# Halving eight products in each of the last three rows of a streamed fp32 matrix product, and moving VectorE's running totals to PSUM

## The chip, the core and the metric

The kernel runs on one core of one Trainium2 chip. The metric is the device time of one execution in microseconds (us), as the median of several runs. A core has the engines TensorE (PE in the profile; its weight loads are PEld), VectorE (DVE), ScalarE (ACT), GpSimd (POOL) and SyncE (SP), which here only issues loads. They run their own instruction lists in order and meet through semaphores. SBUF and PSUM are the on-chip memories; TensorE writes to PSUM alone, which has eight banks of 512 fp32 values in each of 128 partitions.

## The reference

A graph layer with an 8192 x 8192 matrix A and an 8192 x 128 matrix x. The part that the change touches is the first product.

```python
def _lap_mul(A, x):
    d = 1.0 / jnp.sqrt(jnp.sum(A, axis=-1))
    return d[:, None] * (A @ (d[:, None] * x))
z = _lap_mul(A, x) @ W1 + b1
z = jax.nn.leaky_relu(z, negative_slope=0.1)
...
S = jnp.where(ranks < k, S, 0.0)      # similarities of z, the 4 nearest of each row
A2 = S + A
out = _lap_mul(A2, x) @ W2 + b2       # then x + out, layer norm
```

All of it is fp32. A row's scale d is known only when the whole row of A has been summed.

## The kernel before

A comes in 16 x 16 quads of 512 rows x 512 columns, 1 MB each, transposed on the host to tiles of 128 x 4 x 512. The first stage streams all 256 quads through SBUF once, row block by row block (16 quads each; "row b" below is a row block of 512 rows, "quad (b, q)" its columns of block q).

- SP (L665, L666) loads quad after quad into slots of 1 MB. A slot is loaded again once VectorE has added its quad and TensorE has done its product, if it has one. `next_slot` picks the slot; the last twelve loads of the stage (`STREAM_END`) use six slots only.
- VectorE adds the row's 16 quads into `total`, a 128 x 2048 tile in SBUF (`add_quad`, L1481, 15 additions), folds it to 128 x 512 (`add_tiles`, L1486 and L1487), and TensorE finishes the row sum with four matmuls of one column (`row_sums`, L776). VectorE then reads the sums (`read_sums`, L1491), ScalarE takes the root (L1046), and VectorE makes d with a few small instructions (`newton`, L432 to L440) and scales the 512 rows of x (`scale_xs`, L1499). In VectorE's list, `read_sums` of row b-1 stands behind the first addition of row b, and `scale_xs` of row b-1 behind the second.
- TensorE multiplies quad (b, q) by the scaled rows of x as soon as row q's scale is known, which is at once for q < b (`product`, L767, four fp32 matmuls; the trace shows two records for each). The other quads come a second time in the second stage. For rows 13, 14 and 15 the first stage has 14, 15 and 17 products; those of a row go into one PSUM bank.
- The second stage (98 quads, `two`) works with halves: ScalarE rounds a quad to fp32r (`round_2`, L1039), VectorE subtracts (`rest_2`, L1564), and TensorE makes three fp32r matmuls for each tile (L830, L831, L834): high by high, high by low, low by high. It needs the two halves of the scaled x, which ScalarE (`high_half`, L1031) and VectorE (`low_half`, L1505) make during row 15.
- GpSimd does nothing in the first stage.

The stages behind it (similarities, the four nearest, the second product) are unchanged.

```python
pe.wait_ge(ld_a[slot_of[n]], turn_of[n])
pe.wait_ge(xs_ok, q + 1)
...
for i in range(1, B):
    add_quad(b, i)
    if b >= 1 and i == 1:
        read_sums(b - 1)
    if b >= 1 and i == 2:
        scale_xs(b - 1)
    ...
add_tiles(b)
```

Of the kernel before, what the change touches and what calls it, by code (L numbers as in the profile page):

```python
# [27 lines left out]
SLOTS_END = (0, 1, 2, 3, SLOTS_2, SLOTS_2 + B // TB)  # L28
SLOTS_Y = {16: 2 * B // 4, 17: 3 * B // 4}
X_FROM = {14: 2 * B // 4, 15: 3 * B // 4}  # L30
STREAM_END = 12
# [4 lines left out]
LOW_AT = 10  # L36
ROW_BANKS = (2, 0, 3)
# [47 lines left out]

def plan_ab():
# [42 lines left out]
def build(nc, x, at, W1, b1, W2, b2, consts, out, xs_dram, xh_dram, xl_dram, acc_dram):  # L129
# [31 lines left out]
    for n in range(n_one + len(two)):  # L161
        if n < n_one - STREAM_END:
            k = next_slot(n, [*range(SLOTS_A), *(k for k, b in SLOTS_Y.items() if left(n) <= B * (b + 1)),
                              *(k for k, b in X_FROM.items() if left(n) <= B * b)])
# [8 lines left out]
        now[k] = n  # L173
    last_in = {}
# [3 lines left out]
    with ctx:  # L178
# [45 lines left out]
        total = R1[:, N + 2 * SLOT:N + 3 * SLOT]  # L224
# [50 lines left out]
        al_2 = [sb(f"al_2{k}", [P, TB, BC], F32R, at=top_of["R1"] + k * SLOT * 4) for k in range(2)]  # L275
        x_last = sb("x_last", [P, 2, 2, TB, D], F32R, at=over1 + 2 * SLOT * 4)
# [61 lines left out]
        xl_ok = sem("xl_ok")  # L338
        rnd_2 = sem("rnd_2")
# [105 lines left out]
        halves = range(min(q for r, q in two), B)  # L445
# [308 lines left out]
        def _(pe):  # L754
# [3 lines left out]
            def product(b, q):  # L758
# [5 lines left out]
                if first and b >= YB:  # L764
                    pe.wait_ge(y_saved, b - YB + 1)
                for k in range(TB):
                    i = pe.matmul(PS[:, b % YB], xs[:, q * TB + k], slots_a[slot_of[n]][:, k],  # L767
                                  start=first and k == 0, stop=prod_at[b, q] == closed[b] and k == TB - 1)
                i.then_inc(prod1, 1)
# [50 lines left out]
            for n, (b, q) in enumerate(two):  # L820
# [6 lines left out]
                pe.wait_ge(xl_ok, q - halves[0] + 1)  # L827
# [194 lines left out]
        def _(act):  # L1022

            saved = 0
            def high_half(q):
# [7 lines left out]
            def round_2(n):  # L1033
                act.wait_ge(ld_a[slot_of[n_one + n]], turn_of[n_one + n])
                if n < 2:
                    free_of_stage_1(act, SLOTS_B + n)
# [4 lines left out]
            for b in range(B):  # L1041
                if b == B - 1:
                    for q in halves[:-2]:
                        high_half(q)
                act.wait_ge(sums_read, b + 1)
                act.activation(tiny[:, 0, 0:TB], rowsum[:, b * TB:(b + 1) * TB], ACT.Sqrt).then_inc(root_ok, 1)  # L1046
                if b == B - 1:
                    round_2(0)
                    for q in halves[-2:]:
                        high_half(q)  # L1050
                    round_2(1)
                while saved < B and all(q <= b for r, q in flat if r == saved):
                    act.wait_ge(prod1, closed[saved])
                    for k, first in SLOTS_Y.items():
                        if first == saved:
                            free_of_stage_1(act, k)
                    act.activation(R2[:, saved * BC:(saved + 1) * BC], PS[:, saved % YB], ACT.Copy)\
                       .then_inc(y_saved, 1)
                    saved += 1
                if b < B - 1:  # L1060
                    act.wait_ge(xs_ok, b + 1)
# [204 lines left out]
        def _(pool):  # L1266
            def stationary(g, j, first):
# [195 lines left out]
        def _(v):  # L1463
# [8 lines left out]
            def add_quad(b, i):  # L1472
# [7 lines left out]
                other = slots_a[slot_of[n - 1]] if i == 1 else total.rearrange("p (k c) -> p k c", c=BC)  # L1480
                v.tensor_tensor(total.rearrange("p (k c) -> p k c", c=BC), other, slots_a[slot_of[n]], ALU.add)\  # L1481
                 .then_inc(rows_added, 1)

            def add_tiles(b):
                v.wait_ge(rows_added, (B - 1) * (b + 1))
                link(v.tensor_tensor(half, total[:, 0:2 * BC], total[:, 2 * BC:4 * BC], ALU.add))  # L1486
# [21 lines left out]
            for b in range(B):  # L1508
                for i in range(1, B):
# [5 lines left out]
                    if b == B - 1:  # L1515
# [3 lines left out]
                add_tiles(b)  # L1519

            read_sums(B - 1)
# [36 lines left out]
            def rest_2(n):  # L1558
                v.wait_ge(rnd_2, n + 1)
                if n < 2:  # L1560
# [212 lines left out]
```

## Time and profile before

| | us |
|---|---|
| Time, median of 3 runs | 2691.74 (2691.24 to 2696.32) |
| Span of the profiled execution | 2759.5 |
| PE busy in it | 2482.6 (90%) |
| DVE busy | 2319.8 (84%) |
| ACT busy | 1606.7 (58%) |
| POOL busy | 1195.4 (43%) |
| Mean granted TensorE clock | 0.969 |

The span runs from the first to the last instruction of one profiled execution; no other time of that execution is given, and it is 67.8 us longer than the median of the runs without a profile. The busy shares are averages over stages with different limits; the first stage ends at about 720 us of the span. Times of rows below count from the span's start.

### The profile page before, as it was taken

Reading aid. Unit: us, or ns where it says so; the run is one execution under the profiler, and the core shown is the slowest. Engines: PE = TensorE matmul, PEld = TensorE weight load, DVE = VectorE, ACT = ScalarE, POOL = GpSimd, SP = SyncE. Lnnn points to the kernel's source line nnn. Section 1 sums busy time; section 2 is a strip of 40 time slices with the busy share of each in tenths; the row PEclk is TensorE's granted clock in tenths of the full one; section 3 lists DMA queues with packets and bytes.
Section 4 is the critical chain, followed back from the end, with each engine's and each line's share of the span. In section 5 each row is a group of like instructions: output and inputs, shape, how many; then the busy total and the mean of one; then the engine's idle time right before and its main releaser. Section 6 shows DMA issues by size and latency. Waiting matters only on the chain.

```text
span 2759.5 us, 29107 instructions
## 1 busy us (share of the span) xinstructions
PE 2482.6 (90%) x9356; PEld 1722.4 (62%) x9356; DVE 2319.8 (84%) x1411; ACT 1606.7 (58%) x1905; POOL 1195.4 (43%) x987
## 2 busy tenths in 40 slices
PE   1367999999999998899999999999999987888978
PEld 0133444444677776578787877778787764666655
DVE  7998899977788888999999999999999773666766
ACT  0000000000477767999989899899988763555655
POOL 0000000000000000377778878788878956666760
PEclk9688999999999999999999999999999988999989
DMA  9999999995899960146555655555655688988975
GB/s 385 421 402 408 398 421 421 421 421 215 320 349 342 338 226 7 35 141 183 151 163 138 179 142 175 140 170 149 174 143 167 182 309 343 347 324 320 345 295 208
DMA packets 147949, 718.58 MB, mean 260 GB/s; under 512 B 19025, under 2 KB 26961, under 8 KB 86609
## 3 DMA queue, kind: packets, MB, share of 16 engines
q1 hardware_dynamic: 124384, 670.49, 65.6%
q0 software_dynamic: 18800, 37.77, 5.7%
q10 hardware_dynamic: 4608, 8.39, 0.8%
q8 instruction: 79, 1.29, 0.2%
q14 instruction: 78, 0.63, 0.1%
HBM read 680.40 MB, written 36.18 MB: 260 GB/s over the span
## 4 chain that ended last, share of the span: by engine, by line
PE 56%; issue 10%; ACT 10%; DVE 9%; DMA 7%; POOL 3%; another core or an unknown queue 3%; SPq 0%; ACTq 0%; POOLq 0%; DVEq 0%
PE PS L767 17%; PE PS L866 5%; PE PS L868 5%; PE PS L867 5%; DMA ring<-at 4%; ACT R L1141 3%; PE PS L834 3%; PE PS L910 3%; PE PS L921 3%; PE PS L911 3%; PE PS L830 2%; PE PS L831 2%; ACT ah_t L1191 2%; DVE R L1621 2%
## 5 line engine op out<-in xcount | busy, mean ns | idle before, releaser
L1299 POOL TENSOR_TENSOR al<-ring,ah 128x1024 fp32r<-128x1024 f32 x264 | 644.0, 2441 | 180.5 <-ACT ah L1112 168.7
L1621 DVE MAX8 R<-R 128x8 f32<-128x8192 f32 x64 | 555.9, 8685 | 68.1 <-ACT R L1141 67.9
L1141 ACT ACTIVATE R<-PS 128x1024 f32<-128x1024 f32 x512 | 518.1, 1018 | 114.1 <-PE PS L874 83.1
L1624 DVE FIND_INDEX8 R<-R,R 128x8 uint32<-128x8192 f32 x64 | 555.9, 8685 | 0.3 <-issue 0.3
L1272 POOL CAST zst<-zh 128x128 fp32r<-128x128 f32 (+1 forms) x64 | 26.2, 410 | 1113.2 <-DVE zl L1556 811.5
L866 PE MATMUL PS<-zh,zst 128*128 128x512 f32 x1024 | 407.3, 398 | 28.6 <-ACT PS L1127 12.7
L868 PE MATMUL PS<-zh,zst 128*128 128x512 f32 x1024 | 400.4, 391 | 0.0
L867 PE MATMUL PS<-zl,zst 128*128 128x512 f32 x1024 | 400.1, 391 | 0.0
L1456 POOL DMA_INDIRECT R<-xs_dram,R x256 | 279.7, 1093 | 145.2 <-issue 75.5
L1127 ACT ACTIVATE PS<-R 128x1024 f32<-128x1024 f32 x310 | 318.0, 1026 | 6.6
L1046 ACT ACTIVATE tiny<-rowsum 128x4 f32<-128x4 f32 x16 | 3.3, 205 | 481.2 <-DVE rowsum L1491 481.2
L767 PE MATMUL PS<-cache,R 128*128 128x512 f32 x584 | 262.9, 602 | 17.0 <-DMA cache<-at 11.6
L1481 DVE TENSOR_TENSOR R<-R,cache 128x2048 f32<-128x2048 f32 x106 | 242.9, 2292 | 21.2 <-DMA cache<-at 19.0
L866 PEld LDWEIGHTS PS<-zh,zst 128*128 128x128 f32 x1024 | 192.1, 188 | 97.0 <-ACT PS L1127 25.3
L981 PE MATMUL PS<-ah_t,xsh 128*128 128x512 f32 x368 | 162.9, 443 | 63.9 <-ACT ah_t L1191 45.0
L868 PEld LDWEIGHTS PS<-zh,zst 128*128 128x128 f32 x1024 | 192.2, 188 | 41.7
L867 PEld LDWEIGHTS PS<-zl,zst 128*128 128x128 f32 x1024 | 192.3, 188 | 39.8 <-issue 0.7
L767 PEld LDWEIGHTS PS<-cache,R 128*128 128x128 f32 x584 | 112.1, 193 | 157.6 <-issue 144.1
L767 PE MATMUL PS<-ring,R 128*128 128x512 f32 x384 | 177.4, 610 | 11.2 <-DMA ring<-at 5.7
L1564 DVE TENSOR_TENSOR al<-ring,ah 128x2048 fp32r<-128x2048 f32 x66 | 151.0, 2290 | 35.6 <-ACT ah L1039 33.1
L1481 DVE TENSOR_TENSOR R<-R,ring 128x2048 f32<-128x2048 f32 x72 | 165.0, 2292 | 11.5 <-DMA ring<-at 9.6
L1668 DVE TENSOR_TENSOR al_t<-R,ah_t 128x1024 fp32r<-128x1024 f32 x98 | 115.7, 1221 | 63.2 <-ACT ah_t L1191 36.9
(177 smaller groups left out, 4469.9 us busy)
## 6 DMA issues: line engine op xcount, KB each, us to landing
R<-at SPq DMA_DIRECT2D x152, 1024.0 KB, 13.3
ring<-at SPq DMA_DIRECT2D x148, 1024.0 KB, 9.5
ring<-at SPq DMA_DIRECT2D x264, 512.0 KB, 3.9
cache<-at SPq DMA_DIRECT2D x117, 1024.0 KB, 20.2
raw_sq<-at SPq DMA_DIRECT2D x21, 1024.0 KB
raw_z<-at SPq DMA_DIRECT2D x20, 1024.0 KB
raw_ring<-at SPq DMA_DIRECT2D x20, 1024.0 KB
acc_dram<-R POOLq DMA_DIRECT2D x78, 256.0 KB, 5.7
```

The source lines that it names most:

```text
L767: i = pe.matmul(PS[:, b % YB], xs[:, q * TB + k], slots_a[slot_of[n]][:, k], start=first and k == 0, stop=prod_at[b, q] == closed[b] and k ...
L866: pe.matmul(bank, zst[:, par, 0], zh[:, cols], start=not on_seed, stop=False, skip_group_check=True)
L867: pe.matmul(bank, zst[:, par, 0], zl[:, cols], start=False, stop=False, skip_group_check=True)
L868: i = pe.matmul(bank, zst[:, par, 1], zh[:, cols], start=False, stop=on_seed, skip_group_check=True)
L981: pe.matmul(bank, xsh[:, t], ah_t[n % 2][:, k], start=from_zero and k == 0, stop=False, skip_group_check=True)
L1127: act.activation(pair(False, 0, c), sq_row[c], ACT.Copy).then_inc(seeded, 1)
L1141: act.activation(score[j % 2][:, c * EC:(c + 1) * EC].rearrange("p (b c) -> p b c", b=2), pair(first, j, c), ACT.Copy).then_inc(copied, 1)
L1299: pool.tensor_tensor(al[:, k % SPLIT], raw[k % RAW], ah[:, k % SPLIT].bitcast(F32), ALU.subtract)\
L1456: pool.indirect_dma_start(gx[f % 2][:, j, m], None, xs_dram, bass.IndirectOffsetOnAxis(ap=sidx[:, FIN[f] * TB + j, m:m + 1], axis=0))\
L1481: v.tensor_tensor(total.rearrange("p (k c) -> p k c", c=BC), other, slots_a[slot_of[n]], ALU.add)\
L1621: v.max(top[:, j], score[j % 2]).then_inc(dve3, 1)
L1624: v.max_index(place[:, j], top[:, j], score[j % 2]).then_inc(placed, 1)
```

## The change

In rows 13, 14 and 15 (`LATE = 13`) the products of quads with q < 8 (`QL`), 24 in all, are made from halves, as in the second stage: ScalarE rounds the quad (`round_1`), GpSimd subtracts in place (`low_1` lies over the quad's own slot), and TensorE makes three fp32r matmuls a tile. A rounded quad has two buffers, so `round_1` of one waits for the product of the one before last. The subtraction waits for `rows_added`, VectorE's addition of the same quad, since it overwrites it. The order of the loads of these rows mixes plain and halved quads (`mixed`). The high half of x for q < 8 is made by ScalarE in row 12, the low half by GpSimd, in place over the scaled x (`xl_q`); three quads of it are copied later for the second stage (`move_low`).

Four slots are given up from row 12 on (`SLOTS_LATE`: two hold the rounded quads, two the high half of x); the last five loads, not twelve, use few slots. From row 12 on VectorE's running total lies in four PSUM banks; the last addition of a row writes `total` in SBUF. So the products of rows 9 on share three banks instead of seven (`y_bank`). The low halves of x for q of 8 to 13 move behind the last `add_tiles`.

```diff
-STREAM_END = 12
+SLOTS_LATE = (SLOTS_B, SLOTS_B + 1, SLOTS_2, SLOTS_2 + 1)
+STREAM_END = 5
+LATE, TOTAL_AT, QL = 13, 12, 8
...
+def mixed(b):
+    plain, halved = list(range(QL, b)), list(range(QL))
+    order = [plain.pop(0), plain.pop(0)]
+    n_plain, n_halved, taken = len(plain), len(halved), 0
+    while plain or halved:
+        if halved and (QL - len(halved) + 1) * n_plain <= (taken + 1) * n_halved or not plain:
+            order.append(halved.pop(0))
+        else:
+            order.append(plain.pop(0))
+            taken += 1
+    return order
...
-        low = list(range(b))
+        low = list(range(b)) if b < LATE else mixed(b)
...
+            def product_of_halves(b, q, first):
+                m = half_1[b, q]
+                low = low_1[slot_of[load_at[b, q]]]
+                pe.wait_ge(xl_low_q, 4)
+                pe.wait_ge(rnd_1, m + 1)
+                for k in range(TB):
+                    t = q * TB + k
+                    pe.matmul(PS[:, y_bank(b)], xsh[:, t], ah_2[m % 2][:, k], start=first and k == 0, stop=False)
+                    pe.matmul(PS[:, y_bank(b)], xl_q[:, t], ah_2[m % 2][:, k], start=False, stop=False)
+                pe.wait_ge(al_1, m + 1)
+                for k in range(TB):
+                    i = pe.matmul(PS[:, y_bank(b)], xsh[:, q * TB + k], low[:, k], start=False, stop=False)
                 i.then_inc(prod1, 1)
...
+            def round_1(m):
+                n = load_at[halved_1[m]]
+                act.wait_ge(ld_a[slot_of[n]], turn_of[n])
+                if m < 2:
+                    free_of_stage_1(act, SLOTS_B + m)
+                else:
+                    act.wait_ge(prod1, prod_at[halved_1[m - 2]])
+                act.activation(ah_2[m % 2][:, :, :], slots_a[slot_of[n]], ACT.Copy).then_inc(rnd_1, 1)
...
+            pool.wait_ge(prod1, last_whole)
+            for k in range(4):
+                pool.wait_ge(xh_low_q, k // 2 + 1)
+                tiles = slice(k * T // 8, (k + 1) * T // 8)
+                pool.tensor_tensor(xl_q[:, tiles], xs[:, tiles], xsh[:, tiles].bitcast(F32), ALU.subtract)\
+                    .then_inc(xl_low_q, 1)
+            for m, bq in enumerate(halved_1):
+                n = load_at[bq]
+                raw_1 = slots_a[slot_of[n]]
+                pool.wait_ge(rnd_1, m + 1)
+                pool.wait_ge(rows_added, (B - 1) * (n // B) + max(n % B, 1))
+                pool.tensor_tensor(low_1[slot_of[n]][:, :, :], raw_1, ah_2[m % 2][:, :, :].bitcast(F32), ALU.subtract)\
+                    .then_inc(al_1, 1)
...
-                other = slots_a[slot_of[n - 1]] if i == 1 else total.rearrange("p (k c) -> p k c", c=BC)
-                v.tensor_tensor(total.rearrange("p (k c) -> p k c", c=BC), other, slots_a[slot_of[n]], ALU.add)\
+                running = PS[:, 3:3 + TB] if b >= TOTAL_AT else total
+                other = slots_a[slot_of[n - 1]] if i == 1 else running
+                v.tensor_tensor(total if i == B - 1 else running, other, slots_a[slot_of[n]], ALU.add)\
                  .then_inc(rows_added, 1)
...
-                    if b == B - 1:
-                        for k, q in enumerate(halves[:-2]):
-                            if i == LOW_AT + k // 2:
-                                low_half(q)
                 add_tiles(b)
 
+            for q in halves[:-2]:
+                low_half(q)
             read_sums(B - 1)
```

The products of row 13 now stand in this order (q, with the halved ones in brackets, and the diagonal quad (12, 12) of the row before): 8, 9, [0], [1], (12, 12), 10, [2], [3], [4], 11, [5], [6], [7], 12. Row 14: 8, 9, [0], [1], (13, 13), 10, [2], [3], 11, [4], [5], 12, [6], [7], 13. Row 15: 8, 9, [0], 10, (14, 14), [1], [2], 11, [3], 12, [4], [5], 13, [6], row sums, [7], 14, and (15, 15) last.

VectorE's list at the start of row 13, before: `R` holds `total` and the scaled x, `ring` and `cache` the slots, `tiny` and `dsc` the small values of d.

```order
L1481 TENSOR_TENSOR R_49<-cache 128x2048 [waits ld_a7,ld_a13]
L1491 COPY rowsum<-PS 128x4 [waits summed]
L1481 TENSOR_TENSOR R_49<-R_49,cache 128x2048 [waits ld_a8,rows_added]
L440 RECIPROCAL tiny<-tiny 128x4 [waits root_ok,sums_read]
L432 TENSOR_TENSOR tiny<-tiny 128x4 [waits dve]
L433 TENSOR_TENSOR tiny<-tiny,rowsum 128x4 [waits dve]
L435 TENSOR_SCALAR tiny<-tiny 128x4 [waits dve]
L436 TENSOR_TENSOR dsc<-tiny 128x4 [waits dve]
L1499 TENSOR_TENSOR R_49<-R_49,dsc 128x512 [waits s_x13,dve]
L1481 TENSOR_TENSOR R_49<-R_49,cache 128x2048 [waits ld_a9,rows_added]
```

The same place of the changed kernel (its lines are shifted; the addition is L1617, the scaling L1635).

```order
L1617 TENSOR_TENSOR PS<-ring,cache 128x2048 [waits ld_a1,ld_a10]
L1627 COPY rowsum<-PS 128x4 [waits summed]
L1617 TENSOR_TENSOR PS<-PS,ring 128x2048 [waits ld_a2,rows_added]
L484 RECIPROCAL tiny<-tiny 128x4 [waits root_ok,sums_read]
L476 TENSOR_TENSOR tiny<-tiny 128x4 [waits dve]
L477 TENSOR_TENSOR tiny<-tiny,rowsum 128x4 [waits dve]
L479 TENSOR_SCALAR tiny<-tiny 128x4 [waits dve]
L480 TENSOR_TENSOR dsc<-tiny 128x4 [waits dve]
L1635 TENSOR_TENSOR R_49<-R_49,dsc 128x512 [waits s_x12,dve]
L1617 TENSOR_TENSOR PS<-PS,cache 128x2048 [waits ld_a12,rows_added]
```

The order is the same; the additions read one operand from PSUM, but the small ones (L476, L477, L480), the scaling, the first addition of a row and the fold still read two operands from SBUF.

GpSimd's list in the changed kernel, from its first work on (`low` lies over the slot that it reads; before, the list began with the copies at `zst`, in the second stage).

```order
L1390 TENSOR_TENSOR xl_q<-R_49,xsh 128x1024 [waits xh_low_q,prod1]
L1390 TENSOR_TENSOR xl_q<-R_49,xsh 128x1024 [waits xh_low_q] x3
L1397 TENSOR_TENSOR low_88<-ring,ah_81 128x2048 [waits rows_added,rnd_1]
L1397 TENSOR_TENSOR low_94<-cache,ah_82 128x2048 [waits rows_added,rnd_1]
L1397 TENSOR_TENSOR low_90<-cache,ah_81 128x2048 [waits rows_added,rnd_1]
L1397 TENSOR_TENSOR low_91<-cache,ah_82 128x2048 [waits rows_added,rnd_1]
```

All these rows are new: four subtractions of 128x1024 for x and 24 of 128x2048 for the quads, each behind a rounding and behind VectorE's addition of the same quad.

TensorE's list at the start of row 13 of the changed kernel (L837 row sums, L814 fp32 product, L825, L826 and L829 the three parts of a halved one); before, L776 was followed by 14 products of the form L767.

```order
L837 MATMUL PS<-ones,R_49 128x1 x4
L814 MATMUL PS<-cache,R_49 128x512 x4
L814 MATMUL PS<-ring,R_49 128x512 x4
L825 MATMUL PS<-ah_81,xsh 128x512
L826 MATMUL PS<-ah_81,xl_q 128x512
...
L829 MATMUL PS<-low_88,xsh 128x512 x4
```

Two plain products stand in front of the first halved one, whose last four matmuls (L829) need GpSimd's result.

## Rows read from the trace of the kernel before

**Rows 1.** Busy time by windows, core 0, around the end of the first stage.

```profile
core 0: us, PE busy (x) PEld busy (x) DVE busy (x) ACT busy (x) POOL busy (x), PEclk, DMA share, GB/s
560.00:620.00 60.00, 60.00 (x148) 27.00 (x147) 48.29 (x35) 0.80 (x2) 0.00 (x0) 1.00 1.01 421
```

**Rows 2.** Chain that ended last, 500 to 780 us: start, duration, what.

```profile
558.64 48.17 PE PS L767 x112
607.60 51.61 PE PS L767 x120
659.99 20.72 PE PS L767 x48
...
709.39 10.41 PE PS L767 x24
```

**Rows 3.** Timeline of PE, early in the second stage: start, duration, what.

```profile
721.49 1.07 PE L834 MATMUL PS<-al,xsh 128*128 128x512 f32 x4
...
724.21 1.07 PE L834 MATMUL PS<-al,xsh 128*128 128x512 f32 x4
```

**Rows 4.** Groups by line and shape, POOL: count, busy us, mean ns.

```profile
L1299 POOL TENSOR_TENSOR al<-ring,ah 128x1024 fp32r<-128x1024 f32 x264 | 644.0, 2441 | 180.5 <-ACT ah L1112 168.7 <-PE PS L921 1.6 <-POOL d2s L1354 0.6
...
L1442 POOL TENSOR_TENSOR al_t<-R,ah_t 128x2048 fp32r<-128x2048 f32 x2 | 9.1, 4558 | 0.5 <-ACT ah_t L1191 0.5
```

**Rows 5.** Groups by line and shape, ACT, the rounding of a quad.

```profile
L1039 ACT ACTIVATE ah<-ring 128x2048 fp32r<-128x2048 f32 x66 | 126.4, 1915 | 62.3 <-PE PS L834 60.0 <-DMA ring<-at 1.9
```

**Rows 6.** Timeline of DVE, start of row 13 (idle before in brackets).

```profile
558.68 0.16 DVE L1491 COPY rowsum<-PS 128x4 f32<-128x4 f32 x1 [5.56 <-PE PS L776]
558.76 2.29 DVE L1481 TENSOR_TENSOR R<-R,cache 128x2048 f32<-128x2048 f32 x1
...
561.17 0.16 DVE L432 TENSOR_TENSOR tiny<-tiny 128x4 f32<-128x4 f32 x1
```

**Rows 7.** Timeline of DVE, from the scaling to the start of row 14.

```profile
562.69 6.93 DVE L1481 TENSOR_TENSOR R<-R,cache 128x2048 f32<-128x2048 f32 x3
...
592.92 1.23 DVE L1486 TENSOR_TENSOR R<-R 128x1024 f32<-128x1024 f32 x1
594.18 0.69 DVE L1487 TENSOR_TENSOR R<-R 128x512 f32<-128x512 f32 x1
...
607.64 0.16 DVE L1491 COPY rowsum<-PS 128x4 f32<-128x4 f32 x1 [10.56 <-PE PS L776]
```

**Rows 8.** Timeline of POOL in the second stage.

```profile
811.94 2.23 POOL L1272 CAST zst<-zh 128x128 fp32r<-128x128 f32 x1 [811.49 <-DVE zl L1556]
814.12 0.29 POOL L1273 CAST zst<-zl 128x128 fp32r<-128x128 f32 x1
...
814.59 2.35 POOL L1273 CAST zst<-zl 128x128 fp32r<-128x128 f32 x1
```

**Rows 9.** Timeline of DVE at the same time.

```profile
811.72 2.29 DVE L1564 TENSOR_TENSOR al<-R,ah 128x2048 fp32r<-128x2048 f32 x1
814.48 2.30 DVE L1564 TENSOR_TENSOR al<-R,ah 128x2048 fp32r<-128x2048 f32 x1 [0.47 <-ACT ah L1039]
```

**Rows 10.** Timeline of PE around a wait early in the stage.

```profile
268.30 6.09 PE L767 MATMUL PS<-ring,R 128*128 128x512 f32 x8 [3.81 <-DMA ring<-at]
274.23 3.60 PE L767 MATMUL PS<-R,R 128*128 128x512 f32 x8
```

**Rows 11.** Busy time by windows at that wait; the clock stands behind POOL.

```profile
268.00:272.00 4.00, 3.70 (x5) 1.63 (x6) 3.71 (x8) 0.00 (x0) 0.00 (x0) 0.50 1.02 426
```

**Rows 12.** Timeline of SP's queue at the end of row 15.

```profile
697.94 29.31 SPq L666 DMA_DIRECT2D ring<-at  x7
```

**Rows 13.** Timeline of DVE, the last addition of the stage.

```profile
704.02 2.28 DVE L1481 TENSOR_TENSOR R<-R,ring 128x2048 f32<-128x2048 f32 x1
```

**Rows 14.** Groups by line and shape, DVE: operands in SBUF alone, and one in PSUM.

```profile
L1675 DVE TENSOR_TENSOR R<-R,PS 128x512 f32<-128x512 f32 x9 | 6.1, 680 | 0.0
L1505 DVE TENSOR_TENSOR xsl<-R,xsh 128x512 fp32r<-128x512 f32 x9 | 5.8, 684 | 0.0
```

More of the change, by code:

```diff
@@ L83, in held, with y_bank, row_of_y_bank @@
     return range(b - DEFER[b], b)
+def mixed(b):
[9 more added lines that the diff above has]
+    return order
+def y_bank(b):
+    return b % YB if b < 9 else (b + 2) % 3
+def row_of_y_bank(b):
+    return b - YB if b < 12 and b != 10 and b != 11 else b - 3
 def plan_ab():
@@ L162, in build @@
         if n < n_one - STREAM_END:
-            k = next_slot(n, [*range(SLOTS_A), *(k for k, b in SLOTS_Y.items() if left(n) <= B * (b + 1)),
+            k = next_slot(n, [*(k for k in range(SLOTS_A) if n < B * TOTAL_AT or k not in SLOTS_LATE), *(k for k, b in SLOTS_Y.items() if left(n) <= B * (b + 1)),
                               *(k for k, b in X_FROM.items() if left(n) <= B * b)])
@@ L173, in build @@
         now[k] = n
+    order_1 = []
+    for b in range(B):
+        sums_at = len(products[b]) - (SUMS_EARLY if b == B - 1 else 0)
+        order_1 += [(b, q) for b, q in products[b][:sums_at]] + [("sums", b)] + products[b][sums_at:]
+    order_1 += products[B]
+    place_1 = {what: n for n, what in enumerate(order_1)}
+    halved_1 = [(b, q) for b, q in flat if b >= LATE and q < QL]
+    half_1 = {bq: m for m, bq in enumerate(halved_1)}
+    last_whole = max(prod_at[bq] for bq in flat if bq[1] < QL and bq not in half_1)
     last_in = {}
@@ L444, in build @@
         ends = list(itertools.accumulate(sum(r == b for r, q in two) for b in blocks2))
-        halves = range(min(q for r, q in two), B)
+        halves = range(QL, B)
         last_quad = {}
@@ new lines, in _, with after @@
+            for b in range(TOTAL_AT):
+                root_of_row(b)
+                while saved < B and all(q <= b for r, q in flat if r == saved):
+                    save_y(saved)
+                    saved += 1
+            def after(k):
+                return place_1[one[last_in[k]]] + 0.5
+            steps = []
+            for b in range(TOTAL_AT, B):
+                steps.append((place_1["sums", b] + 0.7, "root", b))
+            for b in range(saved, B):
+                steps.append((place_1[flat[closed[b] - 1]] + 0.6, "save", b))
@@ new lines, in _ @@
+            for k in range(2):
+                steps.append((after(SLOTS_2 + k), "high", k))
+            steps.append((after(SLOTS_2 + B // TB + 1), "move", 0))
+            for q in halves[:-2]:
+                steps.append((max(after(SLOTS_2 + k // TB) for k in range(QL, q + 1)) + 2.2 + q / 100, "half", q))
+            for m in range(len(halved_1)):
+                at_m = place_1[halved_1[m - 2]] + 0.5 if m >= 2 else place_1[halved_1[m]] - 3.5
+                steps.append((at_m, "round", m))
@@ new lines, in _ @@
+            for _, what, k in sorted(steps):
+                if what == "root":
+                    b = k
+                    root_of_row(b)
+                    if b == B - 1:
+                        round_2(0)
+                        for q in halves[-2:]:
+                            high_half(q)
+                        round_2(1)
+                if what == "save":
+                    save_y(k)
+                if what == "high":
+                    high_of_low_q(k)
+                if what == "move":
+                    move_low()
+                if what == "half":
+                    high_half(k)
+                if what == "round":
+                    round_1(k)
@@ L1514, in _ @@
                         scale_xs(b - 1)
[L1515 to L1518 removed]
                 add_tiles(b)
+            for q in halves[:-2]:
+                low_half(q)
             read_sums(B - 1)
```

71 lines of the change are left out of this document (46 added, 25 removed).

## The prediction

> **What bounds the kernel now.** I read the time by windows first: around rows 13 and 14 PE is busy for the whole window at full clock, DVE for four fifths, and POOL not at all [rows 1]. Then the chain of waits: from row 13 to the end of the stage it is one run of the products of L767, broken only by row sums, and the second stage's matmuls follow directly [rows 2]. So the stage ends when TensorE has done its products. Row 13 lasts from 558.64 to 607.60, 48.96 us for 14 products; row 14 52.39 us for 15; row 15 from 659.99 to 719.80, 59.81 us for 17. One product is 48.17 / 14 = 3.44 us. VectorE has time to spare in rows 13 and 14: it stood idle for 10.56 us before it could read row 13's sums [rows 7]. In row 15 it has none: the last load is issued at 697.94 [rows 12], its addition starts at 704.02 [rows 13], and the row sums follow without slack. The second stage needs TensorE too, so a microsecond won or lost at the end of the first stage goes through to the end.
>
> **What the change takes away.** A product of halves took 724.21 - 721.49 = 2.72 us in the second stage [rows 3], 0.72 us less than a plain one. For 24 of them that is 17.3 us, if the halves are always there in time. They aren't, I think.
>
> **What it adds.** Rounding takes 1.92 us on ScalarE [rows 5], which has hardly any other work there [rows 1]. GpSimd's subtraction of 128x2048 took 4.56 us [rows 4]. It is the slow part: 24 times 4.56 is 109 us, beside some 144 us of TensorE work in the three rows (161.2 less 17.3). And it can't be spread freely. With two buffers the rounding of the next but one starts only after a product ends, so from the end of one halved product to the last part of the next but one pass 1.9 + 4.6 + 0.2 us for semaphores (estimated from gaps of about 0.1 us in the rows). The last four matmuls of a halved product take about a third of 2.72, 0.91 us; the eight before, 1.81.
>
> The four subtractions for x (2.44 us each, 9.8 in all [rows 4]) start when product (12, 7) is through, four products or 13.8 us before row 12's sums, and GpSimd has no other work until 2.5 us after these; without that cover they would cost their length. The high halves and the copy (4096 + 1536 columns, 5.3 us at the price of a rounding) lie beside products as well. The low halves of x now follow the last fold, six at 0.68 us [rows 14], beside two products (6.2 us) that TensorE still has; uncovered they cost 4.1 us. Of the slots, each load still waits for a product at least five before its own (quad (13, 8) for (12, 6), six before), 17 us, against some 6 from issue to use at the end of row 15 [rows 12, 13]; I charge nothing, and if it failed the price is a load's landing for each late one. The next-stage loads start after products 154 to 156 instead of 153, 155 and 156 and stay ahead.
>
> An addition with its total in PSUM isn't in the trace. With one operand in PSUM VectorE took 680 ns for 512 columns, with all in SBUF 684 [rows 14], so I take 2.29 us as before; the upper bound, reading and writing PSUM costing double, is a rival below.
>
> **The ports.** Here GpSimd and VectorE read SBUF at the same time for the first time in this stage. The trace shows what that does: a copy of 128x128 on GpSimd takes 0.29 us alone, but 2.23 and 2.35 us where VectorE's subtraction with two SBUF operands had just begun, and both end about when that does (814.17 against 814.01, 816.94 against 816.78) [rows 8, 9]. So one engine holds something for the length of an instruction, and the other waits. Whether VectorE waits for GpSimd in the same way no row shows; the bounds are 0 and the rest of a 4.56 us instruction. I take the upper one, as a hold of that kind has no reason to know its owner.
>
> The Trainium skill (SBUF — State Buffer, Who interferes with whom) states it for both directions: a VectorE instruction with two SBUF inputs and a GpSimd instruction that reads SBUF exclude each other, and the second blocks until the first has finished, while one SBUF input doesn't conflict. The trace agrees in the direction that it shows (2.23 us in place of 0.29). By that rule the sum is the one worked out below, by blocking in the shown direction alone it is that of the first rival.
>
> The additions to PSUM read one SBUF operand and are free of it. The small instructions of d, the scaling, the first addition of a row and the fold are not.
>
> **The sum, row by row**, in us from the row's start (the end of the sums before it). VectorE reads the sums and makes the second addition by 2.4 [rows 6]. That releases GpSimd on the row's first halved quad, 2.5 to 7.1. VectorE's next instructions, which make d, begin at 561.17, 2.5 after the start [rows 6]: they meet that subtraction and wait until 7.1. The rest and the scaling take 1.6, so the third addition starts at 8.7 and ends at 11.0; it started at 562.69, 4.1, before [rows 7]. In rows 13 and 14 it is quad [1] that is added third, so its subtraction runs from 11.1 to 15.7. TensorE has done 8, 9 and [0] at 9.6 and the first parts of [1] at 11.4, and waits 4.3.
>
> Row 13 then: [1] ends at 16.7, (12, 12) 20.1, 10 at 23.5, [2] 26.2, [3] 29.0. [4]'s rounding waits for [2]: subtraction 28.4 to 33.0, end 34.0 (a wait of 2.2). 11 ends at 37.4, [5] at 40.1; [6]'s subtraction 37.5 to 42.1, end 43.1. VectorE is through its additions at 39.3 (13 more at 2.33 from 8.7) and waits to fold until 42.1; its 1.2 us put [7]'s subtraction at 43.3 to 47.9, end 48.8 (a wait of 3). 12 ends at 52.3, the sums at 53.1. Against 48.96 that is **4.1 lost**.
>
> Row 14 is the same to [3]; with 11, [4], [5], 12, [6] behind it [7] again ends at 48.8, set by GpSimd, 13 at 52.3, the sums at 53.1: against 52.39, **0.7 lost**.
>
> In row 15 [1] is added fourth: subtraction 13.4 to 18.0, just in time, as 10 and (14, 14) stand ahead. [2] ends at 23.5 after a wait of 1.6, 11 at 27.0, [3] 29.7, 12 at 33.1, [4] 35.9. That frees the slot for the last load, 35.9; 6.1 us later, as before [rows 12, 13], VectorE adds it, at 42.0, and is through at 44.3. TensorE reaches the row sums at 44.8 after [5], 13 and [6]. But [7]'s subtraction holds GpSimd from 42.5 to 47.1, so the fold (1.2 and 0.7 [rows 7]) ends at 49.0: 4.3 of waiting. Sums 50.0, [7] 52.7, 14 at 56.2, (15, 15) 59.6. Against 59.81, **0.2 won**.
>
> Together 4.1 + 0.7 - 0.2 = 4.6 lost; of the 17.3 won by shorter products, all goes into waits.
>
> **The clock.** Three waits of 4.3 us stand in that schedule. In row 7 a wait of 3.81 us was followed by a stretch at a granted clock of 0.50, that is 1.2 GHz, and the product behind it took 5.93 (to 274.23) instead of 3.44 [rows 10, 11]: 2.5 more. If that happens at all three it is 7.5, at none 0. I take two, 5.0.
>
> The forecast is 4.6 + 5.0 = 9.6 us more: 2691.7 + 9.6 = 2701.3. The profile's own span would go from 2759.5 to about 2769; it is 67.8 above the median, but the first stage is set by TensorE at full clock, so I add the difference unscaled.
>
> **Rivals.** *VectorE never waits for GpSimd.* Then d comes at 4 as before, [1]'s subtraction directly follows [0]'s (7.1 to 11.7), and there is no wait of 4 us and no fall of the clock. Everything from [1] on lies 4.1 earlier in rows 13 and 14, and without the fold's delay of 1.2 the rows last 47.9 each, 1.1 and 4.5 won; in row 15 [4] ends 1.6 earlier and the fold isn't held, so the last addition ends at 42.7 and the fold at 44.6 (49.0 above): 55.2, 4.6 won. Together 10.2 faster: 2681.5. For it: the trace shows only GpSimd waiting. Against: the hold lasts for whole instructions. It decides as soon as VectorE's third addition of a row starts before about 5.
>
> *Additions in PSUM cost double*, 4.6 us: 13 to 14 in a row make some 66 us with the rest, against 45 to 52 of products in rows 12 to 14; VectorE becomes the bound and the stage loses some 60 to 80: about 2760. Nothing in the rows on PSUM operands speaks for it, but none writes there.
>
> *The change does nothing*, the products paced by GpSimd and gains and waits even out: my schedule without the clock's falls, 2696.3.
>
> **Chances.** VectorE is held: 0.63, of which no fall of the clock 0.12, one to three 0.51 (2698.8 to 2703.8). VectorE isn't held: 0.31, of which 0.27 win more than 0.2%. PSUM double: 0.04. Anything else: 0.02. A difference under 0.2%, 5.4 us, can't be told from none here. That gives faster 0.27, the same 0.18 (0.12 and 0.04 and the rest), slower 0.55. The range must take in the first rival and all falls of the clock with about 3 us for my schedule's errors: 2680 to 2707; the likeliest case by itself is 2696 to 2707.
>
> **What will show it.** Right: the small VectorE instructions after a row's sums stand 4 us or so apart from the second addition, or one of them lasts that long; PE waits on GpSimd at [1] of rows 13 and 14 and on the fold in row 15; windows at 0.50 behind these waits; rows of about 53, 53 and 60 us. Wrong: the third addition right behind the scaling as before, rows near 48; or additions well over 2.3 us; or GpSimd subtractions far from 4.56.

## The result and the profile after

| | us |
|---|---|
| Time after, median of 4 runs | 2707.26 (2706.78 to 2708.00) |
| Time before, median of 4 runs beside them | 2694.03 (2691.24 to 2696.81) |
| Ratio, 95% interval | 1.0050 (1.0037 to 1.0062) |
| Span of the profiled execution after (its own time 2706.78) | 2705.0 |

The change costs 13.2 us where 9.6 were forecast. The direction and the mechanism came as predicted; the time lies some 6 us above the 2701.3 that was forecast and 0.3 us past the upper end of the range. Of the 6 us, 3.6 are the size of the effect and 2.3 the time before: the forecast was added to 2691.74, the median of three runs, and the median of four is 2694.03. The profiled execution before (span 2759.5) reached the second stage at 719.24 us and that of e4_row15_only below (span 2693.0) at 719.67, so the 66 us between the two lie behind the part that the change touches, and the forecast of 2769 for the span missed by 64 for that reason.

The chain of waits is the place to begin; it answers to [rows 2].

```profile
511.27 44.74 PE PS L814 x104
556.01 0.80 PE PS L837 x8
556.91 0.44 DVE PS L1617
...
559.52 4.38 DVE tiny L477
...
613.83 0.80 PE PS L837 x8
617.34 4.38 DVE tiny L477
```

Row 12, whose totals lie in PSUM but whose products are plain, is still one run of TensorE's products. From row 13 on the chain leaves TensorE: after the row sums (L837) and the end of one addition it goes through one VectorE instruction of 128x4 that lasts 4.38 us. VectorE's timeline at the start of row 13, to be laid beside [rows 6, 7]:

```profile
556.91 2.30 DVE L1617 TENSOR_TENSOR PS<-PS,ring 128x2048 f32<-128x2048 f32 x1
559.12 0.17 DVE L484 RECIPROCAL tiny<-tiny 128x4 f32<-128x4 f32 x1
559.32 0.16 DVE L476 TENSOR_TENSOR tiny<-tiny 128x4 f32<-128x4 f32 x1
559.52 4.37 DVE L477 TENSOR_TENSOR tiny<-tiny,rowsum 128x4 f32<-128x4 f32 x1
564.03 0.17 DVE L479 TENSOR_SCALAR tiny<-tiny 128x4 f32<-128x4 f32 x1
564.23 0.17 DVE L480 TENSOR_TENSOR dsc<-tiny 128x4 f32<-128x4 f32 x1
...
565.04 2.29 DVE L1617 TENSOR_TENSOR PS<-PS,cache 128x2048 f32<-128x2048 f32 x1
```

GpSimd's timeline in row 13:

```profile
559.36 4.51 POOL L1397 TENSOR_TENSOR low<-ring,ah 128x2048 fp32r<-128x2048 f32 x1 [6.25 <-DVE PS L1617]
567.48 13.71 POOL L1397 TENSOR_TENSOR low<-cache,ah 128x2048 fp32r<-128x2048 f32 x3 [3.61 <-DVE PS L1617]
587.84 9.10 POOL L1397 TENSOR_TENSOR low<-cache,ah 128x2048 fp32r<-128x2048 f32 x2 [6.65 <-ACT ah L1137]
596.88 5.60 POOL L1397 TENSOR_TENSOR low<-ring,ah 128x2048 fp32r<-128x2048 f32 x1
602.44 5.01 POOL L1397 TENSOR_TENSOR low<-cache,ah 128x2048 fp32r<-128x2048 f32 x1
```

The subtraction of [0] runs from 559.36 to 563.87. The small instruction L477, with two operands in SBUF, began at 559.52 and ended at 563.89. The third addition starts 8.2 us after the sums (8.7 forecast) and the subtraction of [1] at 567.48. The additions to PSUM took 2.30 us also beside a subtraction, so doubling them is out as a rival. TensorE's timeline shows what the wait did (a plain product shows as 3.60 us; from start to start it is the prediction's 3.44, as its end overlaps the next one):

```profile
567.95 0.39 PE L826 MATMUL PS<-ah,xl_q 128*128 128x512 f32 x1
572.06 2.08 PE L829 MATMUL PS<-low,xsh 128*128 128x512 f32 x4 [3.72 <-POOL low L1397]
573.93 5.63 PE L814 MATMUL PS<-cache,R 128*128 128x512 f32 x8
579.40 3.60 PE L814 MATMUL PS<-ring,R 128*128 128x512 f32 x8
...
607.51 1.20 PE L829 MATMUL PS<-low,xsh 128*128 128x512 f32 x4 [1.96 <-POOL low L1397]
608.54 5.29 PE L814 MATMUL PS<-cache,R 128*128 128x512 f32 x8
...
629.88 2.07 PE L829 MATMUL PS<-low,xsh 128*128 128x512 f32 x4 [3.72 <-POOL low L1397]
631.75 5.73 PE L814 MATMUL PS<-cache,R 128*128 128x512 f32 x8
...
719.65 1.86 PE L837 MATMUL PS<-ones,R 128*128 128x1 f32 x8 [4.15 <-DVE R L1623]
721.38 0.77 PE L825 MATMUL PS<-ah,xsh 128*128 128x512 f32 x1
...
724.87 1.08 PE L829 MATMUL PS<-low,xsh 128*128 128x512 f32 x4
```

Three waits of about 4 us were forecast, at [1] of rows 13 and 14 and at the fold of row 15, and they are there: 3.72, 3.72 and 4.15. Behind each the products are slow, and behind one of 1.96, at [7] of row 13, too. Windows of 8, 8 and 6 us behind the three, with the granted clock in the sixth column (after POOL), answer to [rows 11]. 1.00 is 2.4 GHz and 0.50 is 1.2; a mean between the two says that a part of the window ran at 1.2. Below, a fall is such a drop to 1.2 GHz:

```profile
core 0: us, PE busy (x) PEld busy (x) DVE busy (x) ACT busy (x) POOL busy (x), PEclk, DMA share, GB/s
...
572.00:580.00 8.00, 7.94 (x14) 4.11 (x15) 7.86 (x4) 2.31 (x2) 7.86 (x3) 0.62 0.48 172
...
630.00:638.00 8.00, 8.00 (x14) 4.00 (x15) 7.90 (x4) 2.39 (x2) 8.00 (x2) 0.62 0.40 131
719.00:725.00 6.00, 5.35 (x17) 4.63 (x18) 5.31 (x14) 1.63 (x2) 0.00 (x0) 0.52 0.12 49
```

All kernels below are compared by the length of rows 13 to 15 in TensorE's timeline, from the start of one row's sums to the start of the next (for row 15 to the first matmul of the second stage):

| Kernel | row 13 | row 14 | row 15 | sum | less before | time less before |
|---|---|---|---|---|---|---|
| before | 48.96 | 52.39 | 60.20 | 161.6 | | |
| after | 57.82 | 56.26 | 62.33 | 176.4 | +14.9 | +13.2 |
| e4_row15_only | 48.96 | 52.40 | 61.57 | 162.9 | +1.4 | +3.3 |
| e5_totals_sbuf | 72.73 | 72.12 | 85.30 | 230.2 | +68.6 | +69.2 |
| e1_fill | 57.48 | 52.90 | 59.99 | 170.4 | +8.8 | +5.4 |
| e6_fill_more | 53.90 | 52.94 | 60.02 | 166.9 | +5.3 | +4.4 |
| e2_small_ops_psum | 50.98 | 49.33 | 61.77 | 162.1 | +0.5 | +0.3 |
| e3_fold_psum | 51.90 | 50.34 | 55.66 | 157.9 | -3.7 | -4.1 |
| e8_hold | 48.80 | 48.35 | 55.70 | 152.9 | -8.7 | -8.1 |
| e7_hold_order | 43.84 | 47.28 | 55.65 | 146.8 | -14.8 | -15.2 |
| e9_order_alone | 48.33 | 49.20 | 63.76 | 161.3 | -0.3 | -0.1 |

The two last columns agree within 3.5 us in every line, so the rows hold nearly the whole effect. The rows come from one execution of each kernel and the times are medians, so some of the rest is spread between executions: the sums of row 12 began at 557.69 in the profile of before, and between 555.85 and 558.36 over the changed kernel and its variants, whose products are the same up to there. In e1_fill, where the columns differ most, the profiled execution was the longest of twelve (2704.38, median 2698.80).

### The profile page after: what moved, and what is told of

Read it like the earlier page. It is cut to its first block, busy times and chain, and to the rows that moved or that the text cites. A ratio compares the mean times of both kernels' runs of the same rounds, so it can differ in the third digit from the quotient of the medians.

```text
span 2705.0 us, 29417 instructions
## 1 busy us (share of the span) xinstructions
PE 2458.2 (91%) x9452; PEld 1733.8 (64%) x9452; DVE 2358.0 (87%) x1408; ACT 1656.6 (61%) x1929; POOL 1321.7 (49%) x1015
## 4 chain that ended last, share of the span: by engine, by line
PE 54%; ACT 12%; DVE 11%; issue 10%; DMA 8%; POOL 4%; SPq 0%; ACTq 0%; POOLq 0%; DVEq 0%
PE PS L814 14%; PE PS L930 5%; PE PS L932 5%; PE PS L931 5%; ACT R L1260 4%; DMA ring<-at 4%; PE PS L974 3%; PE PS L898 3%; PE PS L985 3%; PE PS L975 3%; PE PS L1035 3%; PE PS L894 2%; PE PS L895 2%; DVE R L1756 2%; ACT ah_t L1310 2%
## 5 line engine op out<-in xcount | busy, mean ns | idle before, releaser
L1390 POOL TENSOR_TENSOR xl_q<-R,xsh 128x1024 fp32r<-128x1024 f32 x4 | 10.7, 2708 | 541.9 <-PE PS L814 541.9
L814 PE MATMUL PS<-cache,R 128*128 128x512 f32 x496 | 229.6, 614 | 17.8 <-DMA cache<-at 12.4
L1617 DVE TENSOR_TENSOR R<-R,cache 128x2048 f32<-128x2048 f32 x78 | 178.8, 2292 | 18.1 <-DMA cache<-at 16.6
L814 PEld LDWEIGHTS PS<-cache,R 128*128 128x128 f32 x496 | 97.3, 198 | 137.1 <-issue 122.1
L1045 PE MATMUL PS<-ah_t,xsh 128*128 128x512 f32 x368 | 154.4, 419 | 18.2 <-ACT ah_t L1310 18.0
L1104 ACT ACTIVATE ah<-ring 128x2048 fp32r<-128x2048 f32 x66 | 126.4, 1915 | 62.5 <-PE PS L898 60.6
L814 PE MATMUL PS<-ring,R 128*128 128x512 f32 x336 | 154.1, 606 | 10.9 <-DMA ring<-at 5.5
```

The lines of the kernel that those rows point to most:

```text
L814: i = pe.matmul(PS[:, y_bank(b)], xs[:, q * TB + k], slots_a[slot_of[n]][:, k], start=first and k == 0, stop=prod_at[b, q] == closed[b] an ...
L1045: pe.matmul(bank, xsh[:, t], ah_t[n % 2][:, k], start=from_zero and k == 0, stop=False, skip_group_check=True)
L1617: v.tensor_tensor(total if i == B - 1 else running, other, slots_a[slot_of[n]], ALU.add)\
```

## The experiments

**Row 15 alone (e4_row15_only).** Is it the totals in PSUM and the slots that cost, or the halved products of rows 13 and 14?

```diff
-LATE, TOTAL_AT, QL = 13, 12, 8
+LATE, TOTAL_AT, QL = 15, 12, 8
```

> The changed kernel with halved products in row 15 alone (rows 13 and 14 made of plain products; totals in PSUM and slots as in the change). Theory: rows 13 and 14 are as in the kernel before, 49.0 and 52.4, since totals in PSUM cost nothing by themselves; row 15 about 62 as after the change: 2707.3 - 8.8 - 3.9 = 2694.6, no change from the kernel before. Rival: the totals in PSUM or the fewer slots cost something by themselves: rows 13 and 14 over 51 and 54.

Measured: 2696.75 against 2693.45, ratio 1.0012 (1.0003 to 1.0021). Rows 13 and 14 last 48.96 and 52.40, what they lasted before to 0.01 us, so totals in PSUM and fewer slots cost nothing there by themselves. Row 15 lost 1.4 on its own; the other 1.9 of the 3.3 us do not show in the rows, which are those of an execution of 2694.82, 1.9 under the median of its twelve.

**Totals in SBUF (e5_totals_sbuf).** If two operands in SBUF are what excludes GpSimd, every addition must meet it once the totals are in SBUF.

```diff
-                running = PS[:, 3:3 + TB] if b >= TOTAL_AT else total
+                running = total
```

> The changed kernel with the running totals of rows 12 to 15 in SBUF, where those of the rows before lie, and all else as in the change. Theory: an addition then reads two operands from SBUF, and it and a subtraction of GpSimd exclude each other for their whole length. A row holds 14 or 15 additions of 2.3 us and 8 subtractions of 4.56, 69 to 71 us one after the other, beside 56 to 62 now: the three rows last some 213 in place of 176, and the time is about 2744. Rival: VectorE's small instructions were held by something other than the shared access, and additions run beside subtractions as they do now: 2707.

Measured: 2762.57 against 2693.39, ratio 1.0256 (1.0241 to 1.0272). The additions and subtractions whose quads lie in `cache`, over the three rows (count, busy us, mean ns, idle before):

```profile
L1617 DVE TENSOR_TENSOR R<-R,cache 128x2048 f32<-128x2048 f32 x22 | 96.8, 4398 | 0.6
L1397 POOL TENSOR_TENSOR low<-cache,ah 128x2048 fp32r<-128x2048 f32 x14 | 89.8, 6422 | 35.8 <-DVE R L1617 35.7
```

An addition lasts 4.40 us in the mean in place of 2.30 and a subtraction 6.42 in place of 4.5: each engine waits for the other. The loss is larger than expected: against the changed kernel 55 us were lost where 37 were expected, and the rows came out at 72.7, 72.1 and 85.3, 230 in place of some 213 together. Rows 13 and 14 are near the 69 to 71 of serial work; in row 15 TensorE waits 9.44 for the fold as well.

**No waiting of VectorE (e2_small_ops_psum).** The small operands of d go to PSUM, so that no instruction of the chain reads two operands from SBUF (the reciprocal is made twice, in SBUF and in PSUM, and each instruction takes one operand from either).

```diff
-newton(link, rowsum[:, cols], ..., tiny[:, 1, 0:TB], tiny[:, 2, 0:TB], dsc[:, cols])
...
+y0_p, a, d = (PS[:, YB, k * TB:(k + 1) * TB] for k in (8, 9, 10))
...
+link(v.tensor_tensor(a, y0_p, y0, ALU.mult))
+link(v.tensor_tensor(a, a, r, ALU.mult))
...
-v.tensor_tensor(xs[:, cols], xs[:, cols], bcast(dsc[:, cols], D), ALU.mult)
+v.tensor_tensor(xs[:, cols], xs[:, cols], bcast(d, D), ALU.mult)
```

> The changed kernel, with the small operands of d (root's reciprocal, two steps, d itself) in PSUM as well for rows 12 to 15, so that none of these instructions, nor the scaling of x, reads two operands from SBUF; one reciprocal and one copy more, some 0.4 us. Theory: the 4.37 us that the small instruction lasts after a row's sums is GpSimd's subtraction holding what two SBUF operands need; without it the third addition starts about 4.4 after a row's start in place of 8.2, the wait at [1] and the fall of the clock behind it go, and the fold is still held. Rows 13 and 14 about 49 each (57.8 and 56.3 now), row 15 some 60: about 17 less, 2690. Rival: VectorE is held there by something else (a semaphore's turn, or any use of SBUF): third addition at 8 as now, 2707 or a little more.

Measured: 2693.70 against 2693.45, ratio 0.9997 (0.9989 to 1.0006). VectorE's timeline at the start of row 13:

```profile
561.64 0.17 DVE L1640 TENSOR_TENSOR PS<-PS,tiny 128x4 f32<-128x4 f32 x1
561.85 0.17 DVE L1641 TENSOR_TENSOR PS<-PS,rowsum 128x4 f32<-128x4 f32 x1
...
563.14 2.29 DVE L1617 TENSOR_TENSOR PS<-PS,cache 128x2048 f32<-128x2048 f32 x1
```

The instruction that lasted 4.37 (here L1641) lasts 0.17 beside the same subtraction, which runs from 561.61. The third addition starts 4.2 after the row's start in place of 8.2, the wait at [1] shrinks from 3.72 to 0.20, and the product behind it takes 3.60. Rows 13 and 14 are 13.8 us shorter than after the change. Expected were 49 each and 2690 in all: row 13 still has a wait of 2.48 at [7], and a product of 5.29 behind it, and row 15 lasts 61.77 for some 60, which together are the 3.7 us that the time is over.

**The fold too (e3_fold_psum).** As in the experiment before, and the last addition of a row is made in two parts, of which one stays in PSUM.

```diff
+                if b >= TOTAL_AT and i == B - 1:
+                    link(v.tensor_tensor(running[:, 0:2], running[:, 0:2], slots_a[slot_of[n]][:, 0:2], ALU.add))
+                    v.tensor_tensor(total[:, 2:4], running[:, 2:4], slots_a[slot_of[n]][:, 2:4], ALU.add)\
+                     .then_inc(rows_added, 1)
+                    return
...
+                if b >= TOTAL_AT:
+                    v.tensor_tensor(PS[:, 3], PS[:, 3], total[:, 2], ALU.add).then_inc(dve, 1)
...
+                    link(v.tensor_tensor(half[:, 0:BC], PS[:, 4], total[:, 3], ALU.add))
+                    v.tensor_tensor(part, PS[:, 3], half[:, 0:BC], ALU.add).then_inc(part_ok, 1)
+                    return
```

> As e2_small_ops_psum, and the fold of rows 12 to 15 reads one operand from PSUM and one from SBUF too: the last addition is made in two parts, one left in PSUM, and the fold is three instructions of 512 columns. Theory: the fold is no longer held by GpSimd, nor does it stretch a subtraction. Row 15's wait of 4.15 ahead of the sums and the fall behind it (2.6) go, rows 13 and 14 end some 1 us earlier each: about 2682, under the kernel before, as the rival in the prediction in which VectorE never waits. Rival: TensorE reaches row 15's sums before the last load is added in any case, or the last subtractions pace the rows: as e2_small_ops_psum, 2690.

Measured: 2689.37 against 2693.45, ratio 0.9986 (0.9978 to 0.9995). Row 15 gave 6.1 of the 6.8 expected, 61.77 to 55.66; its sums wait 0.55 in place of 4.15. Rows 13 and 14, expected some 1 us shorter, grew by 0.9 and 1.0, and the time is 7.4 over the 2682 expected. The timelines of GpSimd and VectorE show why:

```profile
590.93 4.66 POOL L1397 TENSOR_TENSOR low<-ring,ah 128x2048 fp32r<-128x2048 f32 x1
596.00 6.12 POOL L1397 TENSOR_TENSOR low<-cache,ah 128x2048 fp32r<-128x2048 f32 x1 [0.41 <-ACT ah L1137]
...
593.99 3.75 DVE L1624 TENSOR_TENSOR PS<-cache 128x2048 f32<-128x2048 f32 x1
```

The earlier fold let the next row's first addition, both operands of which lie in SBUF, come earlier too, and it held the last subtraction of the row: the hold had moved.

**Hold the first addition (e8_hold).** On top of the experiment before, the first addition of rows 14 and 15 waits for the last subtraction of the row before it.

```diff
+                if b > LATE and i == 1:
+                    v.wait_ge(al_1, QL * (b - LATE))
```

> As e3_fold_psum, and the first addition of rows 14 and 15, whose two operands lie in SBUF, waits until GpSimd's last subtraction of the row before is through. VectorE stood idle for some 11 us behind that addition. Theory: the last subtraction took 6.12 and 6.61 us because that addition held it for 1.5 and 2.0; without it the waits at [7], 3.52 and 1.92, shrink by so much, and the fall of the clock in row 13 (1.7) goes: rows 13 and 14 at 48.7 and 48.4 in place of 51.9 and 50.3, 2684. Rival: the addition is late for the next row, or the wait at [7] is GpSimd's start and not its length: 2689.

Measured: 2685.30 against 2693.39, ratio 0.9972 (0.9962 to 0.9982). Rows of 48.80 and 48.35, expected 48.7 and 48.4. The subtraction is back at its own length:

```profile
597.74 4.57 POOL L1397 TENSOR_TENSOR low<-cache,ah 128x2048 fp32r<-128x2048 f32 x1 [0.44 <-ACT ah L1137]
```

**Another order (e7_hold_order).** The same as e8_hold, with plain (p) and halved (h) quads of rows 13 and 14 in another order.

```diff
+HALVED = {13: 'pphhhphhphphh', 14: 'pphhphhphphhph'}
+    if b in HALVED:
+        return [(halved if c == "h" else plain).pop(0) for c in HALVED[b]]
```

> As e8_hold, with another order of plain and halved quads in rows 13 (two plain, [0] to [2], plain, [3], [4], plain, [5], plain, [6], [7]) and 14 (two plain, [0], [1], plain, [2], [3], plain, [4], plain, [5], [6], plain, [7]), so that GpSimd's 4.56 us a quad are spread over the row. Theory: what is left of the waits is GpSimd's pace against the order; by the steps of the prediction without the holds, row 13 lasts about 44.5 and row 14 47.5 (48.7 and 48.4 in e8_hold), 5 less: 2679. Rival: with rows of 44 us VectorE's additions or the loads set the pace, and 1 or 2 us are won: 2683.

Measured: 2678.18 against 2693.39, ratio 0.9949 (0.9935 to 0.9962): faster than both kernels, and 0.8 from the number expected. TensorE's waits for GpSimd over the three rows were 15.4 us after the change; in this kernel's list of waits (in total, times, longest) they are

```profile
PE PS L842 <- DVE R L1640: 0.5, 1, 0.5
...
PE PS L834 <- POOL low L1402: 0.4, 2, 0.2
```

**Order alone (e9_order_alone).** The changed kernel with rows 13 and 14 in the orders pphphhphhhphh and pphphphhphhphh.

> The changed kernel with another order of plain and halved quads in rows 13 (two plain, [0], plain, [1], [2], plain, [3] to [5], plain, [6], [7]) and 14 (two plain, [0], plain, [1], plain, [2], [3], plain, [4], [5], plain, [6], [7]), and nothing else: VectorE's small instructions and the fold read SBUF as in the change and are held as before. Theory: the hold of 4.4 us comes from where these instructions stand, and stays; what it costs is the wait at [1] and the fall of the clock behind it, and with a plain product between [0] and [1] both go: by the steps of the prediction rows 13 and 14 last 48 to 49 each in place of 57.8 and 56.3, row 15 as in the change, 2690. Rival: the hold delays all that VectorE adds, and the wait moves to the next quad: rows of 52 or more, 2698.

Measured: 2693.00 against 2693.07, ratio 1.0002 (0.9993 to 1.0011). VectorE's small instruction lasts as long as ever:

```profile
562.03 4.36 DVE L482 TENSOR_TENSOR tiny<-tiny,rowsum 128x4 f32<-128x4 f32 x1
```

But [1] now comes a plain product later, and the rows last 48.33 and 49.20, as expected. A hold of 4.4 us costs what stands unhidden behind it. Row 15 came out 1.4 longer than after the change, which is half of what the time misses of the 2690 expected: TensorE waited 1.54 in place of 1.03 at [2], and behind the wait for the fold, 4.16 here, the slow work lasted longer (the low part of [7] took 1.91 in place of 1.08).

**Is it idleness that drops the clock (e1_fill, e6_fill_more)?** The changed kernel, with matmuls of 256 columns into an unused corner of PSUM where TensorE waits.

```diff
+FILL = {(13, 1): 30, (13, 7): 14, (14, 1): 30, ('sums', 15): 30}
...
+                fill((b, q))
                 pe.wait_ge(al_1, m + 1)
...
+            def fill(what):
+                for k in range(FILL.get(what, 0)):
+                    pe.matmul(PS[:, YB, BC // 2:BC], xsh[:, 0], xsh[:, 0:2], start=True, stop=True)
...
+                fill(("sums", b))
                 pe.wait_ge(part_ok, b + 1)
```

> The changed kernel, with matmuls of 256 columns into an unused corner of PSUM issued where TensorE stands waiting: 30 each ahead of the low part of [1] in rows 13 and 14 (waits of 3.72 us) and ahead of the sums of row 15 (4.15), 14 ahead of the low part of [7] in row 13 (1.96). They take less time than the waits, so the schedule of the other engines is unchanged. Theory: the granted clock falls because TensorE stands idle there, and the four falls cost 4.7 us in row 13, 3.1 in row 14 and 2.6 in row 15. Then row 13 lasts 53.1, row 14 53.2, row 15 59.3 in place of 57.8, 56.3 and 61.9, the low part of [1] is followed by a product of 3.6 rather than 5.6, and the time is 2707.3 - 10.4 = 2697. Rival: the slow products come with the switch between the kinds of product, or with the waits themselves being longer than forecast, whatever TensorE does in them: rows and time as after the change, 2707.

Measured: 2698.80 against 2693.45, ratio 1.0019 (1.0010 to 1.0027). Rows 14 and 15 came to 52.90 and 59.99, and the product behind [1] in row 13 took 3.59. But row 13 kept its length, and the time is 1.8 over the 2697 expected. With [1] on time, TensorE waited 2.18 at [4] and 2.19 at [7] behind its 14 matmuls, and a plain product behind each took 5.29. At [4]:

```profile
591.57 1.19 PE L831 MATMUL PS<-low,xsh 128*128 128x512 f32 x4 [2.18 <-POOL low L1404]
592.60 5.29 PE L815 MATMUL PS<-ring,R 128*128 128x512 f32 x8
```

So both were filled:

```diff
-FILL = {(13, 1): 30, (13, 7): 14, (14, 1): 30, ('sums', 15): 30}
+FILL = {(13, 1): 30, (13, 4): 16, (13, 7): 31, (14, 1): 30, ('sums', 15): 30}
```

> As e1_fill, with matmuls also ahead of the low part of [4] in row 13 (16 of them, 2.0 us for a wait of 2.18), and 31 ahead of that of [7] (there were 14, and 2.19 us of waiting left). Theory: the two falls that were left in row 13 of e1_fill, each of which made a plain product 5.29 in place of 3.60, go; row 13 lasts 57.5 - 3.4 = 54.1, the rest as in e1_fill, 2698.8 - 3.4 = 2695.4. Rival: GpSimd paces the row's last products, and the time won at one wait is waited at the next: row 13 at 56 or more, 2697 to 2699.

Measured: 2697.74 against 2693.39, ratio 1.0022 (1.0013 to 1.0031). Row 13, at 53.90, has the value that the theory gave (54.1). The time does not: it is 2.3 over the theory's 2695.4 and in the range of the rival, 2697 to 2699. The theory had taken the 3.4 us that row 13 of the longest execution of e1_fill could lose off the median of twelve, and against that median 1.1 us were won. So in the profiled executions the added fillings take two falls away; how often e1_fill has those falls is not known. TensorE's timeline in row 13:

```profile
569.49 3.75 PE L836 MATMUL PS<-xsh 128*128 128x256 f32 x30
573.47 1.19 PE L831 MATMUL PS<-low,xsh 128*128 128x512 f32 x4 [0.23 <-POOL low L1404]
574.50 3.60 PE L815 MATMUL PS<-cache,R 128*128 128x512 f32 x8
...
603.01 3.88 PE L836 MATMUL PS<-xsh 128*128 128x256 f32 x31
606.72 1.09 PE L831 MATMUL PS<-low,xsh 128*128 128x512 f32 x4
607.65 3.59 PE L815 MATMUL PS<-cache,R 128*128 128x512 f32 x8
```

The window behind [1], to be laid beside that of 572 to 580 above:

```profile
573.00:581.00 8.00, 7.78 (x24) 3.81 (x22) 7.86 (x5) 2.51 (x2) 7.95 (x3) 1.00 0.54 187
```

GpSimd's result comes no sooner than after the change (573.47 against 572.06, with the row 1.3 later), and the product behind it takes 3.60 in place of 5.63, at a granted clock of 1.00. Ahead of [1] the one thing that differs is what TensorE did while it waited, so it is the idle wait that the fall follows.

## Why the prediction was right in kind and short in size

**VectorE is held by GpSimd (right).** 4.37 us in rows 13 to 15, at the instruction named. e2_small_ops_psum takes the two SBUF operands away and the hold goes; e5_totals_sbuf gives it to all additions. The Trainium skill (SBUF — State Buffer, Who interferes with whom) states that both directions exclude, and that one SBUF operand is free of it; the trace agrees, with 4.37 and 0.17 us for the same instruction with two and with one.

**The schedule of the rows (right, within a microsecond).** Forecast without the clock: 53.1, 53.1, and row 15 0.2 shorter than before, +4.6 in all. With the waits filled: 53.90, 52.94, and 0.2 shorter (60.02 against 60.20): +5.3. The time of that kernel, 2697.7, stands beside the 2696.3 that the prediction gave for its schedule with no fall of the clock (2698.0 from the time before measured beside it). One step of its working has a slip, on which nothing hangs: 13 additions of 2.33 us from 8.7 end at 39.0, not 39.3.

**The clock (the step that failed).** "Three waits of 4.3 us stand in that schedule. [...] If that happens at all three it is 7.5, at none 0. I take two, 5.0." It happened at all three, and a fourth time behind [7] of row 13, a wait of 1.96 which the schedule had at 3 and which was not counted. Priced from the timeline after: at [1] in row 13, 2.08 - 1.20 and 5.63 - 3.60, 2.9; in row 14, 2.07 - 1.20 and 5.73 - 3.60, 3.0; behind [7], 5.29 - 3.60 = 1.7; in row 15 the sums took 1.86 in place of 1.05 and the first eight matmuls of [7] 3.49 (721.38 to 724.87) in place of 1.81, 2.5. Together 10.1. By experiment it is 176.4 - 166.9 = 9.5 in the rows, and 2707.26 - 2697.74 = 9.5 in time; what makes up the 0.6 between was not tried. So the term was mis-sized, 5.0 for about 9.5; with it the sum would have been 14.1 for 13.2 measured. The 10.1 are 5.1 above the term, for three reasons: one of the three falls left out (2.5), the fourth not counted (1.7), and a price of 2.5 that is a slow product alone, where the low part of [1] before it was slow as well (0.9 over the three). Taking two of three as a middle had no row behind it: the one wait of that length in the trace [rows 10, 11] had been followed by a fall. So had longer ones of the kernel before, which the prediction did not use. TensorE's timeline there:

```profile
218.83 1.87 PE L776 MATMUL PS<-ones,R 128*128 128x1 f32 x8 [5.50 <-DVE R L1487]
226.12 6.68 PE L767 MATMUL PS<-cache,R 128*128 128x512 f32 x8 [5.42 <-DVE R L1499]
```

Five waits of 5.35 to 5.42 us for a row's scale, early in the first stage, were each followed by a product of 5.30 to 6.73 in place of 3.60, and four of the row sums, after waits of 5.50 to 11.41 us for the fold, took 1.87 in place of 1.05. Those rows spoke for three falls of three, 7.5.

**The rivals.** That VectorE never waits did not happen, but its terms could be tried: with the holds of the small instructions, the fold and the first addition taken out one after another, the time went to 2693.7, 2689.4 and 2685.3. Against before that is 8.1 us less; the rival had 10.2, since its rows of 47.9 came to 48.80 and 48.35. In row 15 it had 4.6 won, and 4.5 were. Additions at double cost: 2.30 us, no. That the change does nothing: no.

**Where the 17.3 us of shorter products went.** Into waits for GpSimd, as the prediction said, and into the falls that follow them. Nearly all of it was to be had: e7_hold_order wins 15.2 us over the kernel before with the same 24 halved products.

## What to carry to other kernels

When work moves to GpSimd, list every VectorE instruction beside it that reads two operands from SBUF, the tiny ones first: an instruction of 0.17 us that others wait for can come to 4.4, and one operand in PSUM frees it. Freeing one instruction lets the next come earlier and collide in turn, so look at the whole row again after each step. A wait of TensorE is to be charged with its own length and with the slow products behind it, some 2.5 to 3 us here for waits of about 4; another order of the same products, or holding an instruction that has slack, can be worth more than the shorter products themselves.

## What was not expected of the hardware

Whether a wait is followed by a fall is not told by its length alone. Behind each of the eight waits of 2.48 to 4.16 us in rows 13 to 15 of the kernels with totals in PSUM (three of them after the change), and behind the one of [rows 10], the work was slow: a plain product of 4.3 to 6.1 us, or sums of 1.35 to 1.87 in place of 1.05. Of ten waits of 1.92 to 2.20 us in rows 13 and 14 of these kernels, three were followed by a plain product of 5.29 us (at [7] after the change, at [4] and [7] with the first filling) and seven by one of 3.60. At [4] of row 13 both happened, 2.18 with a fall and 2.19 without; with the totals in SBUF a wait of 1.96 was followed by 5.29, and one of 2.25 by matmuls at full speed. What decides between them was not tried, and stays open.
